# Storing the output batch by batch inside layer 3's stage, and clearing layer 0's sorted lists later in the first stage

## The reference

```python
x = L0_attn_x
xn = _layernorm(x, axis=-1)
x = x + _L0_attn_ref(xn, ...) + _L0_ffn_ref(xn, ...)
...
xn = _layernorm(x, axis=-1)
x = x + _L3_attn_ref(xn, ...) + _L3_ffn_ref(xn, ...)
return x
```

```python
h2 = _rmsnorm(x, gamma2)
gate = jax.nn.softmax(h2 @ Wg + bg, axis=-1)
combined = jnp.einsum('btd,edf,bte->btf', h2, We, gate)
return x + combined
```

## Time and profile before

| | us |
|---|---|
| median of 3 runs | 3681.34 |
| the three runs | 3669.57, 3681.34, 3688.97 |
| the profiled execution | 3657.16 |
| its span, first to last instruction | 3655.4 |
| busy in the span: PE, DVE, ACT, POOL | 3090.9, 2249.9, 1342.0, 1433.4 |
| mean granted TensorE clock | 0.916 |

### The profile page before, as it was taken

One profiled execution on the slowest core, in us unless ns is written; L12 is line 12 of the kernel. 1 busy time (PEld: TensorE's weight loads), 2 busy tenths in 40 slices (PEclk: granted clock), 3 DMA queues, 4 the chain that ended last, 5 costly groups with the idle time before them and its releaser, 6 DMA issues. The chain is left out here.

```text
span 3655.4 us, 46338 instructions
## 1 busy us (share of the span) xinstructions
PE 3090.9 (85%) x14645; PEld 1858.8 (51%) x14645; DVE 2249.9 (62%) x6591; ACT 1342.0 (37%) x3038; POOL 1433.4 (39%) x995
## 2 busy tenths in 40 slices
PE   6849995777859998899999999699999668888895
PEld 3426663555535555444444545476666445555552
DVE  3569998888654442456666665522223488888883
ACT  3425553222236664334334433122332333333321
POOL 1337000345625443022121111224005588888880
PEclk9879998888979999999999998779999779999997
DMA  9346443222230000000000000312223100000001
GB/s 326 117 155 220 128 128 116 75 81 75 75 119 1 1 1 16 26 7 18 18 18 18 18 13 12 118 47 86 91 82 96 66 0 1 1 1 1 1 1 46
DMA packets 137834, 221.06 MB, mean 60 GB/s; under 512 B 12672, under 2 KB 106112, under 8 KB 136832
## 3 DMA queue, kind: packets, MB, share of 16 engines
q1 hardware_dynamic: 98784, 146.92, 12.1%
q0 software_dynamic: 18432, 50.36, 4.3%
q10 hardware_dynamic: 20384, 20.84, 1.6%
HBM read 107.45 MB, written 110.62 MB: 60 GB/s over the span
## 5 line engine op out<-in xcount | busy, mean ns | idle before, releaser
L2206 DVE CUSTOM_DVE_ANT_0 a_ps_s<-a_ps_s,a_hide_row,a_fmax 128x384 f32<-128x384 f32 (+3 forms) x512 | 249.3, 554 | 170.4 <-PE a_ps_s L1913 170.2
L3409 POOL TENSOR_TENSOR c_prod<-c_q,c_k 128x2048 f32<-128x2048 f32 x64 | 292.8, 4601 | 23.2 <-DVE c_y L3460 23.2
L2118 POOL TENSOR_SCALAR_AFFINE_SELECT a_probs<-a_probs 128x512 f32<-128x512 f32 x128 | 80.0, 637 | 561.9 <-ACT a_probs L2395 561.9
L3409 POOL TENSOR_TENSOR c_prod<-c_att,c_v 128x2048 f32<-128x2048 f32 x64 | 289.5, 4560 | 0.0
L1414 POOL TENSOR_TENSOR a_probs<-a_probs,a_causal 128x512 f32<-128x512 f32 (+1 forms) x96 | 157.6, 1654 | 215.2 <-ACT a_probs L1643 215.2
L3304 PE MATMUL c_side<-c_w_e,c_h2T 128*128 128x512 f32 x512 | 231.4, 609 | 2.5 <-DVEq L3603 2.5
L1643 ACT ACTIVATE a_probs<-a_ps_s 128x512 f32<-128x512 f32 (+1 forms) x384 | 170.7, 537 | 119.7 <-PE a_ps_s L1283 119.7
L2395 ACT ACTIVATE a_probs<-a_ps_s 128x512 f32<-128x512 f32 (+1 forms) x384 | 171.8, 537 | 89.4 <-PE a_ps_s L1935 88.9
L695 PE MATMUL p_side<-p_w_expert,p_sortedT 128*128 x636 | 175.7, 399 | 0.0
L3304 PEld LDWEIGHTS c_side<-c_w_e,c_h2T 128*128 128x128 f32 x512 | 100.2, 197 | 126.0 <-issue 122.1
L2774 POOL DMA_INDIRECT b_rows<-y_scratch,b_slot_int x64 | 62.9, 983 | 240.3 <-issue 240.3
(11 more groups left out here) (477 smaller groups left out, 7359.9 us busy)
## 6 DMA issues: line engine op xcount, KB each, us to landing
p_sorted_in<-sorted_scratch SPq DMA_DIRECT2D x39, 512.0 KB, 4.8
y_scratch<-p_y_out SPq DMA_DIRECT2D x39, 512.0 KB, 3.2
sorted_scratch<-all_zero ACTq DMA_DIRECT2D x1, 12160.0 KB, 78.2
sorted_scratch<-all_zero SPq DMA_DIRECT2D x1, 9088.0 KB, 29.7
b_sorted_in<-sorted_scratch SPq DMA_DIRECT2D x17, 512.0 KB, 4.5
y_scratch<-b_y_out SPq DMA_DIRECT2D x17, 512.0 KB, 3.2
sorted_scratch<-all_zero ACTq DMA_DIRECT2D x1, 8192.0 KB, 31.5
all_x_res<-x SPq DMA_DIRECT2D x8, 512.0 KB, 4.9
```

Source lines behind the costliest of these rows:

```text
L2206: last = nc.vector.tensor_tensor_reduce(out=there, in0=there, in1=hide_row[:, (TT - 1 - t) * P:], scale=HD ** -0.5, scalar=fmax[i % 2][:, ...
L3409: nc.gpsimd.tensor_tensor(out, left[:, heads].broadcast_to([P, HALF, HEADS, HD]), right.broadcast_to([P, HALF, HEADS, HD]), ALU.mult).then ...
```

## The change

Layer 3's SP program stores each batch of `x_res` when its experts are added, in eight transfers of 512 KB, and waits for all of them at the end of the stage. The stage `store_output` is removed. In stage one, ACT no longer issues the two clears at the start but one behind `results(1)` and one behind `results(5)`.

```diff
+CLEAR_BEHIND = (1, 5)
...
         @block.scalar
         def _(act):
             act.wait_ge(keep.always, 1)
-            for n, (first, last) in enumerate(((0, LIST_AT[1]), (LIST_AT[1], TILES0))):
+
+            def clear_list(n):
+                first, last = (0, LIST_AT[1], TILES0)[n:n + 2]
                 act.dma_start(io.sorted0_scratch[P * first:P * last].rearrange("(a p) d -> p a d", p=P),
                               keep.zero[:].rearrange("p (a d) -> p a d", a=1).broadcast_to([P, last - first, D])
                               ).then_inc(keep.zeroed0[n], DMA)
+
             act.wait_ge(cols_in, ONE + DMA)
...
                 results(i)
+                if i in CLEAR_BEHIND:
+                    clear_list(CLEAR_BEHIND.index(i))
             decays(B - 1)
...
-        expert_added = room.sem("expert_added")
+        expert_added, stored = room.sem("expert_added"), room.sem("stored")
...
             sp.dma_start(w_e[:], io.l3_w_e).then_inc(experts_in, DMA)
+            for i in range(B):
+                sp.wait_ge(expert_added, ONE + 2 * TILES * (i + 1))
+                sp.dma_start(io.out[i], x_res[:, batch(i), :]).then_inc(stored, DMA)
+            sp.wait_ge(stored, ONE + DMA * B)
...
         layer3(nc, io, keep)
-        store_output(nc, io, keep)
...
-def store_output(nc, io, keep):
-    with ExitStack() as stack:
-        room = Room(nc, stack, "out")
-        stored = room.sem("stored")
-        block = room.block()
-
-        @block.sync
-        def _(sp):
-            sp.dma_start(io.out.rearrange("b p t d -> p b t d"),
-                         keep.x_res[:].rearrange("p (b t) d -> p b t d", b=B)).then_inc(stored, DMA)
-            sp.wait_ge(stored, ONE + DMA)
```

## The result

| | before | changed |
|---|---|---|
| median of 5 runs beside each other, us | 3680.54 (3669.57 to 3688.97) | 3648.23 (3633.88 to 3661.42) |
| ratio of the runs, 95% interval | | 0.9894 (0.9857 to 0.9932) |
| the profiled execution, us | 3657.16 | 3661.42 |
| span and granted clock of it | 3655.4, 0.916 | 3659.7, 0.909 |

The forecast was 3659.8 us, 21.5 us under the median of before. Measured in this comparison are 32.3 us less, and 25.9 us (3676.49 against 3650.57) in a second one further down. One of the 30 runs of the kernel before in that second comparison took 10521.96 us and is left out of its ratios. Yet the profiled execution of the changed kernel took 4.3 us *more* than that of before. The second oddity sits in layer 3, away from both edits, and the same thing makes executions of every one of these kernels differ, by enough for the first; the experiments come to it.

A forecast was written before the change was run, and what follows sets the result against it. TensorE was busy 85%, but the prediction blamed the edges: ACT held by its second clear at the start, 16.0 us without arithmetic at the end. 11.9 + 10.1 - 0.5 = 21.5 us off 3681.34 gave 3659.8 us, range 3640 to 3680.

The forecast's parts named there:

- The first hT, 10.86 us from the hold, the table load hidden: Start of stage one: first hT moves from 33.98 to 23.12 us; gain 9.6 if the 1.28 us table load is exposed.
- The loads 1.0 us sooner: Start of stage one: without clears beside them, DVE's wait for cols ends 1.0 us sooner, bounds 0 and 1.8.
- It carries to the end: After the start: the 11.9 us won there reaches the end, as later steps are released by one another.
- ACT is held by the second transfer behind the first: Start of stage one: ACT's second clear queues behind the first, its issue taking 26618 ns against 422 ns.
- The moved clears are hidden: Stage one, behind silu of batches 1 and 5: issues of 0.42 us fit ACT's idle 1.15 and 6.47 us.
- Collisions, 0.5 us: Late stage one and stage two's start: clears beside saves, w_expert's load, SP's issues and scatters cost 0.5 us, range 0 to 12.3.
- Rival A: Stage one: the moved clear slows POOL's scatters, taking back 12.3 us; gain 9.7, 3671.6 us, chance 0.10.
- Rival B: Stage one: ACT is held for each clear's length even with an empty queue; 3717.8 us, slower, chance 0.04.
- C: Both edges gain less: table load exposed, loads no sooner, store 5.9 us, no barrier saved; 3665.8 us, chance 0.14.
- D: After stage one: the shifted start runs into something that holds, leaving only the end's 10.1 us; 3671.2 us, chance 0.05.
- The store, 10.1 us: End of layer 3: 11.8 us landing becomes 2.6, barriers save 0.93, other seven stores cost nothing; gain 10.1 us, bounds 5.9 and 10.1.
- The sum, and the median: Whole kernel: 11.9 + 10.1 - 0.5 = 21.5 us, taken off the median of 3681.34, giving 3659.8 us.

The follow-up runs named there:

- second comparison: The changed kernel timed once more, unaltered, beside the kernel before: median 3650.57 us against 3676.49, ratio 0.9933.
- the two halves: The kernel before with only the clears moved (3665.03 us, ratio 0.9974), and with only the store moved (3668.28 us, ratio 0.9972).

## Why the prediction was right

**The first hT, 10.86 us from the hold, the table load hidden.** This step failed in its one choice: the table load stands behind the wait in the trace, 1.28 us exposed, as the lower bound had it. I had read "hidden" from a load at 45.68 that stood ahead of its wait, and one row does not tell where the next load stands. What decides it was not found; an activation of one element ahead of the wait did take the load off the path (21.14).

**The loads 1.0 us sooner.** Mis-sized: it is 2.3 us (PE's turn of hn ends at 20.76 in place of 23.08), over the upper bound of 1.8. cols land after 3.4 us; I had priced them by the 4.3 us of a 512 KB load. ACT then follows PE in 0.18 us, not 0.04. The two large errors cancel by luck: 10.86 + 1.0 = 11.9 against 10.86 - 1.28 + 2.32 - 0.14 = 11.8.

**It carries to the end.** Right in sum, not in course. The gain fell to 10.7 us at batches 1 to 3 and rose to 12.4, for reasons that vary from one execution to the next. Over eight traces its mean is 11.7 us, against the 11.4 (11.9 - 0.5) of the forecast.

**ACT is held by the second transfer behind the first.** Right, and shown by both clears behind batch 1 (20.61 us for the two issues) and by one clear at the start (0.42 us).

**The moved clears are hidden.** Right: 0.40 and 0.37 us of issue, both while ACT still worked on silu, so not even its idle time was needed. The first landed after 31.9 us (forecast 31.5); the second ended at 213.2, between 196 and 218.

**Collisions, 0.5 us.** Rival A is refuted: scatters of 0.96 us, root 11.85 us sooner. Saves land after 6.1 us (xn_scratch) and 4.5 us (v_scratch) at the median of 55 to 240 us, as feared, and cost nothing that I can see: the stage's last vector instruction gained 12.42 us. The sentence behind rival A, that all issuers share the 16 DMA engines (the Trainium skill, "Trainium Kernel Development and Optimization", Key Constraints), agrees with these longer landings (2.6 us for both before, in the same stretch), but sharing cost GpSimd's issues nothing. Rival B, ACT held by a clear on an empty queue, falls with the 0.40 and 0.37 us. C came true in one of its parts, the exposed table load, and falls with the rest. D falls too: layer 1 began 13.4 us sooner.

**The store, 10.1 us.** Right to the tenth: 16.0 us behind the last vector instruction became 5.9. The landing took 2.7 us (forecast 2.6). The estimate of 3.2 us, from the section on the anatomy of one DMA in the Trainium skill, "DMA: Bandwidth & Descriptors", was too long; that section fits transfers issued by GpSimd, and this one is SP's. What is left besides the landing went from 16.0 - 11.8 = 4.2 us to 5.9 - 2.7 = 3.2, so the barriers gave 1.0 (forecast 0.93). That the other seven stores cost nothing is shown by 21 more that cost nothing.

**The sum, and the median.** 21.5 us forecast; 22.5 at the edges in the trace; 25.9 and 32.3 in the two comparisons of medians, 19.9 from the two halves. I allowed some 10 us for the spread of the runs and knew nothing of its cause. It was larger than the change's uncertainty in every term. A sign of it was in the trace of before: an instruction of 0.69 us at its shortest with a mean of 2.12. That the measured medians lie on the far side of the forecast, and not on the near one, is chance as far as the runs show: the forecast's ratio is inside the interval of one comparison and outside that of the other.

## What to carry to other kernels

Before a second large transfer is issued on a compute engine, see that the first has landed: the issue of one costs 0.4 us, that of the next 20 to 27. A one-off at either edge (a hold at the start, a store of everything at the end) was worth its full length here, since nothing lay beside it. Where executions of one kernel differ, compare the means of each line between a short and a long one: here a VectorE instruction with two SBUF operands beside GpSimd's products cost more than both edges together, and on GpSimd, with its consumer's queue put in order, it costs little, and the runs agree within 0.1%.

## What the runs showed of the hardware that I had not expected

- A VectorE instruction with two SBUF operands can wait through several GpSimd instructions in a row: 11.63 us over three products, 16.48 us over four, while reductions of one operand keep their 2.28 us.
- The hold of the second clear is shorter in the middle of the stage (20.61 us for both issues) than at its start (27.07), with the same first transfer of 8192 KB, which also landed sooner (26.2 us against 31.5). In both places ACT comes free shortly before the first transfer has landed: 5.6 us in the middle, 4.4 at the start.
- One clear on ACT's queue slows SP's issues as well: 1.51 us for w_gate beside it, 0.43 without.
- A table load can stand behind its activation's wait or ahead of it. In the changed kernel the load at 20.94 stands behind the wait for PE, and so do those at 1516.76 and 2335.63; the ones at 35.01, 152.20 and 238.61 (the first of stage two) stand ahead. What decides it is open.
